# Row maximum of two steps ahead placed in front of the lower half of the probabilities, on VectorE, in the steps that make no scores

## The chip, the cores and the metric

One core of one Trainium2 chip runs the whole program. The metric is the device time of one execution in microseconds (us). Three executions of the kernel before took 634.48, 625.78 and 636.51 us: median 634.48. "Faster" and "slower" below mean by more than 2%.

## The reference, cut to what matters

A gated cross attention is followed by a gated feed-forward part. The attention is where the change lies:

```python
x = rmsnorm(layernorm(x)); q = x @ wq.T; k = ctx @ wk.T; v = ctx @ wv.T      # 16 heads of 32
attn = einsum('blhd,bmhd->bhlm', q, k) * 32**-0.5
attn = where(mask, attn, -inf); attn = softmax(attn)
out = einsum('bhlm,bmhd->blhd', attn, v) @ wo.T
x = x + tanh(g_xattn) * sigmoid(x @ wg.T) * out
```

x is 16 batches of 100 tokens by 512; the context has 361 rows for each batch, of which this path of the kernel reads the last 96 (the mask lets only those through; it looks first whether that holds). The feed-forward part has 1408 hidden units, with weights kept as 4-bit codes that VectorE decodes during the attention.

## The kernel before, in words

The 16 batches are taken in 4 groups of 4. The attention of a group is 16 **steps**, one for each head; a step is done for the 4 batches at once. Groups 0 to 2 from step 6 on, with steps 0 to 5 of the next group, are one pass of a loop that runs three times (called a cycle here); steps 0 to 5 of group 0 stand ahead of it, steps 6 to 15 of group 3 behind it. Each engine has its own list of instructions in the order written and goes through it in that order; semaphores alone tie the engines.

For head n = 16g + i, `step(g, i)` does on each engine:

- TensorE: transposes the probabilities of head i (`bank<-ident,probs`, L1584, three instructions; it waits for `exp` of head i and for `pT_lo` of the step before), multiplies the transposed probabilities of head i-1 by the values (`attend`, L1597, nine instructions; it waits for `pT_lo` of i-1 and for `o` of i-2), in steps with i % 4 == 2 makes the scores of the four heads that follow at i+2 to i+5 (`scores`, L1563 and L1573), and then runs the step's jobs from the table `BESIDE`.
- ScalarE: `probsT_hi` (L880) copies the transposed probabilities rounded to `pT_hi`; `exp_step` (L872, `probs<-bank,nmax`, four instructions) makes the exponentials of head i+2, for which it needs the row maximum `nmax` of that head; then the upper halves of the jobs (`vb_hi`, `kT_hi`, `qT_hi`, `xT_hi`, `oT_hi`).
- VectorE: `probsT_lo` (L1127) makes `pT_lo`, what the rounding left over; `attn_norm` (L1135 `rinv`, L1137 `o`) divides the result of head i-1; `row_max` (L1122, `nmax`) takes the negated row maximum of head i+2; `decode` pieces (`words`, `fp`, `left`, `scale`); then the lower halves of the jobs (`kT_lo` and so on), each of which waits for its upper half from ScalarE.

Each of TensorE's products is done in three passes (hi*hi, hi*lo, lo*hi), which is why every operand has two halves. `scores` writes banks 2 to 5. Before it does so it waits for what used each bank last; for bank 2 that is a job T (turned `o`) whose last reader is `oT_lo`, and in steps 14 and 2 for bank 3 a job X or B (`vb_lo`). A job's name says what it is: X turned tokens, Q, K projections, A and B values, G gate, T turned attention result, O output projection.

In the last group, steps 11 to 15 also run the first tiles of the feed-forward part (L1693 on TensorE, `part_gate` and `part_up` on ScalarE L959 and VectorE L1320). Their products go to the scores' banks 2 to 4, and each bank is opened when `exp` of the head that last held it is done (`open_bank_of`).

The `row_max` of a step reads scores that were made in a step with i % 4 == 2, for heads i+2 to i+5: in that same step only the first of the four is taken, in the three steps that follow the other three.

Of the kernel before, what the change touches and what calls it, by code (L numbers as in the profile page):

```python
# [22 lines left out]
HPG = HEADS // HG  # L23
# [37 lines left out]
def build(nc, x, ctx_tail, ctx_full, mask, mask_tail, g_xattn, g_ffn, norm_w, wq, wk, wv, wo, wg,  # L61
          packed, gu_scales, dn_scales, identity, shifts, x1_dram, gu_dram, dn_dram, out):
    es = ExitStack()
    with es:
# [277 lines left out]
        LOOP_FROM, AHEAD, SCORES_AT = 6, 2, 2  # L342
# [71 lines left out]
        def beside(g, i):  # L414
            jobs = [(g + (i >= LOOP_FROM and IN_STEPS.index(n) >= IN_STEPS.index("X0")), n) for n in BESIDE[i]]
            return [job for job in jobs if exists(*job)]

        def step_ahead(g, i):
            g, i = (g, i + AHEAD) if i + AHEAD < STEPS else (g + 1, i + AHEAD - STEPS)
            return [(g, i)] if not isinstance(g, int) or g < GROUPS else []  # L420
# [8 lines left out]
        def last_step(g, i):  # L429
            return (g, i - 1) if i else (g - 1, STEPS - 1)  # L430
# [638 lines left out]
        def _(dve):  # L1069
# [50 lines left out]
            def row_max(g, i):  # L1120
                dve.wait_ge(s_sc, STEPS * g + i + 1)
                nc.vector.tensor_reduce(nmax[:, i % 4, :], SC[i % HPG][0:L, 0:KC].rearrange("t (b k) -> t b k", b=NB),  # L1122
                                        AXIS_X, ALU.max, negate=True).then_inc(s_max, 1)

            def probsT_lo(g, i):
                dve.wait_ge(s_pthi, STEPS * g + i + 1)
                nc.vector.tensor_tensor(pT[i % 2][LO][:, :, :].rearrange("k c t -> k (c t)"), PT[:, 0:CHUNKS * L],  # L1127
                                        pT[i % 2][HI][:, :, :].rearrange("k c t -> k (c t)").bitcast(F32), ALU.subtract)\
                  .then_inc(s_ptlo, 1)
# [21 lines left out]
            def step(g, i, last=False, cycle=None):  # L1151
                def dequant(place):
                    if cycle is not None:
                        for q, stage in DECODE_AT.get((i, place), ()):
                            decode(cycle, q, stage)

                probsT_lo(g, i)
                dequant(0)
                if not isinstance(g, int) or g or i:
                    attn_norm(*last_step(g, i))  # L1160
                for ahead in step_ahead(g, i):
                    row_max(*ahead)
                dequant(1)
                if not last:
                    for b in NORM_AT.get(i, ()):
                        layer_stats(g + 1, b)
                if last and i == STATS_AT:
                    for m in range(3):
                        ffn_stats(0, m)
                for c, name in beside(g, i):  # L1170
                    if name[0] == "O":
                        output(c - 1, int(name[1]))
                    elif name[0] != "G":
                        job_lo(c, name)
                if not last:
                    for b in NORM_AT.get(i - 1, ()):
                        normalise(g + 1, b)
                dequant(2)
                if last and i in NORMED_AT:
                    if i == min(NORMED_AT):  # L1180
                        dve.wait_ge(s_ctxlo, KT * GROUPS)
                    ffn_normalise(0, NORMED_AT[i])
                if last and i in TURNED_AT:
                    mT_lo(0, TURNED_AT[i])
                if last and i in FIRST_AT:
                    ffn_tile(0, FIRST_AT[i])
# [681 lines left out]
```

## Time and profile before

| | us |
|---|---|
| three executions | 625.78, 634.48, 636.51 |
| median | 634.48 |
| profiled execution, span from first to last instruction | 633.5 |
| TensorE busy | 586.4 |
| VectorE busy | 467.0 |
| ScalarE busy | 324.2 |
| mean granted TensorE clock, share of full speed | 0.936 |

The profiled execution is one execution. Its own time is known as its span; it is 1.0 us below the median of the three. The attention takes the first 375 us or so of it, the rest is the feed-forward part, in which no instruction that the change moves is left. TensorE's busy time is modelled, since its matmuls overlap: a short wait of it can be hidden in it. In a timeline row the number in square brackets is how long the engine stood idle just before, and behind the arrow is what ended the wait.

### The profile page before, as it was taken

How to read it: one execution, taken by the hardware profiler on the slowest of the kernel's cores; microseconds unless marked ns; L12 is line 12 of the kernel's file. 1: busy time of each engine (PE TensorE's matmuls, PEld its weight loads, DVE VectorE, ACT ScalarE, POOL GpSimd, SP SyncE). 2: the span in 40 equal slices, each digit the busy share in tenths (PEclk: the TensorE clock that was granted, in tenths of full speed). 3: DMA queues.
4: the chain of work that ended last, by engine and by line, in shares of the span. 5: the costliest groups of instructions: out<-in, count | busy, mean ns of one | idle time of the engine just before them, and what ended most of it. 6: DMA issues, size and time to landing. Idle time of an engine off the chain costs nothing.

```text
span 633.5 us, 12518 instructions
## 1 busy us (share of the span) xinstructions
PE 586.4 (93%) x4154; PEld 516.0 (81%) x4154; DVE 467.0 (74%) x1063; ACT 324.2 (51%) x872; POOL 227.3 (36%) x244
## 2 busy tenths in 40 slices
PE   3988999999999999998998889899999998999996
PEld 2888878888789788887887877788888897899983
DVE  6466977857877579686655698899889789877731
ACT  4665454433454434553345563666765665666620
POOL 6811130001120001300000363576766676776730
PEclk9787987999897899897999799899999999999999
DMA  7910135232344321342258002820111210011010
GB/s 236 319 70 1 64 129 166 100 103 78 124 128 157 92 78 50 119 121 99 78 194 304 4 2 79 300 74 20 57 34 34 76 35 0 35 35 34 34 60 29
DMA packets 27900, 59.38 MB, mean 94 GB/s; under 512 B 3657, under 2 KB 5833, under 8 KB 27849
## 3 DMA queue, kind: packets, MB, share of 16 engines
q1 hardware_dynamic: 27848, 58.76, 28.3%
q8 instruction: 24, 0.39, 0.3%
q14 instruction: 28, 0.22, 0.1%
HBM read 39.62 MB, written 19.14 MB: 93 GB/s over the span
## 4 chain that ended last, share of the span: by engine, by line
PE 53%; DVE 23%; ACT 9%; issue 8%; POOL 5%; DMA 0%; DVEq 0%; SPq 0%; ACTq 0%; POOLq 0%
PE bank L1693 14%; PE bank L317 11%; PE bank L1706 11%; PE bank L1545 5%; PE bank L1573 3%; PE bank L1597 3%; ACT probs L872 3%; PE bank L1549 3%; DVE pT_lo L1127 2%; DVE vb_lo L1090 2%; POOL hT_lo L753 2%; DVE part_gate L1320 2%; DVE nmax L1122 2%; DVE hidden L1335 1%; PE bank L1584 1%
## 5 line engine op out<-in xcount | busy, mean ns | idle before, releaser
L1693 PE MATMUL bank<-mT_hi,wgu 128*128 128x320 f32 x440 | 142.2, 333 | 14.4 <-DVE part_up L1320 4.9
L1693 PE MATMUL bank<-mT_lo,wgu 128*128 128x320 f32 x440 | 135.3, 318 | 0.0
L872 ACT ACTIVATE probs<-bank,nmax 100x96 f32<-100x96 f32 x256 | 66.2, 341 | 124.0 <-DVE nmax L1122 123.9
L1693 PEld LDWEIGHTS bank<-mT_hi,wgu 128*128 128x128 f32 x440 | 85.7, 195 | 28.4 <-DVE part_up L1320 7.8
L1693 PEld LDWEIGHTS bank<-mT_lo,wgu 128*128 128x128 f32 x440 | 86.1, 196 | 3.4
L760 POOL TENSOR_TENSOR part_gate<-part_gate 128x320 f32<-128x320 f32 x55 | 57.0, 1037 | 80.7 <-DVE part_gate L1320 80.7
L959 ACT ACTIVATE part_up<-bank,scale 128x320 f32<-128x320 f32 x110 | 57.3, 521 | 48.6 <-PE bank L1693 48.5
L1320 DVE SCALAR_TENSOR_TENSOR part_up<-bank,scale,part_up 128x320 f32<-128x320 f32 x110 | 58.5, 545 | 19.9 <-ACT part_up L959 17.0
L959 ACT ACTIVATE part_gate<-bank,scale 128x320 f32<-128x320 f32 x110 | 52.2, 528 | 28.4 <-PE bank L1693 27.6
L1320 DVE SCALAR_TENSOR_TENSOR part_gate<-bank,scale,part_gate 128x320 f32<-128x320 f32 x110 | 55.3, 543 | 13.9 <-ACT part_gate L959 11.3
L766 POOL TENSOR_TENSOR part_up<-part_up 128x320 f32<-128x320 f32 x55 | 57.0, 1037 | 23.6 <-DVE part_up L1320 22.1
L703 POOL TENSOR_TENSOR rstd<-var,halfpow 100x1 f32<-100x1 f32 x16 | 9.2, 573 | 144.0 <-DVE var L1112 143.9
L1706 PE MATMUL bank<-wdn_lo,hT_hi 128*128 128x512 f32 (+1 forms) x143 | 56.6, 396 | 0.0
L1706 PE MATMUL bank<-wdn_hi,hT_lo 128*128 128x512 f32 (+1 forms) x143 | 56.5, 395 | 0.0
L1706 PE MATMUL bank<-wdn_hi,hT_hi 128*128 128x512 f32 (+1 forms) x143 | 56.4, 395 | 0.0
L753 POOL TENSOR_TENSOR hT_lo<-hidden,hT_hi 128x320 fp32r<-128x320 f32 x55 | 49.5, 899 | 4.8 <-ACT hT_hi L973 3.9
L1597 PE MATMUL bank<-vb_hi,pT_hi 128*100 128x68 f32 x192 | 50.8, 265 | 0.0
L1597 PE MATMUL bank<-vb_lo,pT_hi 128*100 128x68 f32 x192 | 50.7, 264 | 0.0
L1597 PE MATMUL bank<-vb_hi,pT_lo 128*100 128x68 f32 x192 | 50.6, 264 | 0.0
L1122 DVE TENSOR_REDUCE nmax<-bank 100x4 f32<-100x384 f32 x64 | 35.2, 549 | 6.8 <-PE bank L1573 6.8
L1127 DVE TENSOR_TENSOR pT_lo<-bank,pT_hi 128x300 fp32r<-128x300 f32 x64 | 29.9, 467 | 7.7 <-ACT pT_hi L880 6.8
L1090 DVE TENSOR_TENSOR vb_lo<-bank,vb_hi 32x256 fp32r<-32x256 f32 (+2 forms) x56 | 23.6, 422 | 16.2 <-ACT vb_hi L852 15.4
(145 smaller groups left out, 1498.0 us busy)
## 6 DMA issues: line engine op xcount, KB each, us to landing
gate_up_scratch<-left SPq DMA_DIRECT2D x12, 512.0 KB, 5.4
down_scratch<-left SPq DMA_DIRECT2D x12, 512.0 KB, 3.8
wgu<-gate_up_scratch SPq DMA_DIRECT2D x11, 512.0 KB, 7.6
words<-in_packed SPq DMA_DIRECT2D x18, 256.0 KB
xn<-in_x SPq DMA_DIRECT2D x16, 200.0 KB
xa<-in_x SPq DMA_DIRECT2D x16, 200.0 KB
x_scratch<-gate SPq DMA_DIRECT2D x16, 200.0 KB
ctx_raw<-in_ctx_tail SPq DMA_DIRECT2D x4, 768.0 KB, 7.8
```

Of the source, the lines that this page charges most:

```text
L317: last = nc.tensor.matmul(out_ap, lhs(a, t), rhs(b, t), start=t == 0 and p == 0, stop=t == tiles - 1 and p == 2)
L753: nc.gpsimd.tensor_tensor(hT[t][LO][:, cols], hidden[n % 2][:, :], hT[t][HI][:, cols].bitcast(F32), ALU.subtract)\
L760: nc.gpsimd.tensor_tensor(a[:, :], a[:, :], b[:, :], ALU.add).then_inc(s_gate_sum, 1)
L766: nc.gpsimd.tensor_tensor(a[:, :], a[:, :], b[:, :], ALU.add).then_inc(s_up_sum, 1)
L872: last = nc.scalar.activation(probs[i % 2][:, cols], SC[i % HPG][0:L, cols], ACT.Exp, bias=nmax[:, i % 4, b:b + 1])
L959: nc.scalar.activation(part[n % 2][i][k][:, :], product_bank(j, t, i, k)[:, 0:TG], ACT.Copy, scale=scale32[:, t, i, k:k + 1]).then_inc(s_e ...
L1122: nc.vector.tensor_reduce(nmax[:, i % 4, :], SC[i % HPG][0:L, 0:KC].rearrange("t (b k) -> t b k", b=NB), AXIS_X, ALU.max, negate=True).the ...
L1127: nc.vector.tensor_tensor(pT[i % 2][LO][:, :, :].rearrange("k c t -> k (c t)"), PT[:, 0:CHUNKS * L], pT[i % 2][HI][:, :, :].rearrange("k c ...
L1320: nc.vector.scalar_tensor_tensor(onto, product_bank(j, t, i, k)[:, 0:TG], scale32[:, t, i, k:k + 1], onto, ALU.mult, ALU.add).then_inc(s_e ...
L1597: last = nc.tensor.matmul(PV[0:L, VW * c:VW * c + 2 * VW].rearrange("t (b w) -> t b w", w=VW), pT[i % 2][ph][:, c, :], vb[vh][:, c, :, VW ...
L1693: last = nc.tensor.matmul(product_bank(j, t, i, k)[:, 0:TG], wgu[t][:, k, 128 * i:128 * i + 128], mT[j % 2][half][:, k, :], start=half == ...
L1706: last = nc.tensor.matmul(bank[6 + slot][0:rows, :], hT[c][a][:, cols], wdn[c][b][:, :], start=c == 0 and p == 0, stop=c == FT - 1 and p == 2)
```

## The change

In steps with i % 4 != 2 (`SCORES_AT` is 2, `HPG` is 4) VectorE now runs `row_max` ahead of `probsT_lo`; before, it ran behind `attn_norm`. In steps with i % 4 == 2 it stays where it was. Nothing is added or taken away, and no other engine's list changes.

```diff
+                if i % HPG != SCORES_AT:
+                    for ahead in step_ahead(g, i):
+                        row_max(*ahead)
                 probsT_lo(g, i)
                 dequant(0)
                 if not isinstance(g, int) or g or i:
                     attn_norm(*last_step(g, i))
-                for ahead in step_ahead(g, i):
-                    row_max(*ahead)
+                if i % HPG == SCORES_AT:
+                    for ahead in step_ahead(g, i):
+                        row_max(*ahead)
                 dequant(1)
```

The first place is VectorE in the loop, steps 12 and 13 (`nmax` is the row maximum, `pT_lo` the lower half, `fp`, `words` and `left` are decoding). Before:

```order
L1099 TENSOR_TENSOR kT_lo<-bank,kT_hi 128x384
L1127 TENSOR_TENSOR pT_lo<-bank,pT_hi 128x300
L1135 RECIPROCAL rinv<-bank 100x4
L1137 TENSOR_TENSOR o<-bank,rinv 100x4x32
L1121 REGISTER_ALU
L1122 TENSOR_REDUCE nmax<-bank 100x4
L1243 REGISTER_ALU
L1249 CAST left<-fp 128x1024
L1227 TENSOR_SCALAR words<-words,shift 128x512
L1085 REGISTER_ALU
L1096 SCALAR_TENSOR_TENSOR qT_lo<-bank,qT_hi 128x400
L1127 TENSOR_TENSOR pT_lo<-bank,pT_hi 128x300
```

With the change (lines below the edit are four further down):

```order
L1099 TENSOR_TENSOR kT_lo<-bank,kT_hi 128x384
L1121 REGISTER_ALU
L1122 TENSOR_REDUCE nmax<-bank 100x4
L1127 TENSOR_TENSOR pT_lo<-bank,pT_hi 128x300
L1135 RECIPROCAL rinv<-bank 100x4
L1137 TENSOR_TENSOR o<-bank,rinv 100x4x32
L1247 REGISTER_ALU
L1253 CAST left<-fp 128x1024
L1231 TENSOR_SCALAR words<-words,shift 128x512
L1085 REGISTER_ALU
L1096 SCALAR_TENSOR_TENSOR qT_lo<-bank,qT_hi 128x400
L1121 REGISTER_ALU
```

The row maximum moved past three instructions, to the place right behind the job of the step before; the decoding and the jobs stand in the same order as they did.

The second place is VectorE in the last group, step 12, beside the first feed-forward tiles (`part_gate`, `part_up`, `hidden`). Before:

```order
L1328 SCALAR_TENSOR_TENSOR hidden<-tgate,part_gate 128x320
L1127 TENSOR_TENSOR pT_lo<-bank,pT_hi 128x300
L1135 RECIPROCAL rinv<-bank 100x4
L1137 TENSOR_TENSOR o<-bank,rinv 100x4x32
L1122 TENSOR_REDUCE nmax<-bank 100x4
L1320 SCALAR_TENSOR_TENSOR part_gate<-bank,scale,part_gate 128x320 x2
```

With the change:

```order
L1332 SCALAR_TENSOR_TENSOR hidden<-tgate,part_gate 128x320
L1122 TENSOR_REDUCE nmax<-bank 100x4
L1127 TENSOR_TENSOR pT_lo<-bank,pT_hi 128x300
L1135 RECIPROCAL rinv<-bank 100x4
L1137 TENSOR_TENSOR o<-bank,rinv 100x4x32
L1324 SCALAR_TENSOR_TENSOR part_gate<-bank,scale,part_gate 128x320 x2
```

Here it moved past the wait of `rinv` for TensorE's `attend` as well, behind which it stood before.

## Rows read from the trace of the kernel before

**Rows 1.** The page, part 1: busy time of each engine, its share, instructions.

```profile
PE 586.4 (93%) x4154; PEld 516.0 (81%) x4154; DVE 467.0 (74%) x1063; ACT 324.2 (51%) x872; POOL 227.3 (36%) x244
```

**Rows 2.** Waits of TensorE, whole span: total us, times, longest us.

```profile
PE bank L1563 <- DVE oT_lo L1101: 8.6, 9, 1.4
PE bank L1563 <- DVE vb_lo L1090: 3.1, 4, 1.6
PE bank L1584 <- DVE pT_lo L1127: 2.0, 1, 2.0
```

**Rows 3.** Waits, 60 to 365 us: ScalarE's exponentials.

```profile
ACT probs L872 <- DVE nmax L1122: 114.5, 57, 3.2
```

**Rows 4.** Timeline of VectorE, third cycle: start, us, [idle before].

```profile
262.33 0.47 DVE L1127 TENSOR_TENSOR pT_lo<-bank,pT_hi 128x300 fp32r<-128x300 f32 x1 [0.56 <-ACT pT_hi L880]
...
268.96 0.57 DVE L1096 SCALAR_TENSOR_TENSOR qT_lo<-bank,qT_hi 128x400 fp32r<-128x400 f32 x1 [0.49 <-ACT qT_hi L858]
...
270.25 0.55 DVE L1122 TENSOR_REDUCE nmax<-bank 100x4 f32<-100x384 f32 x1
...
272.29 0.57 DVE L1101 TENSOR_TENSOR oT_lo<-bank,oT_hi 128x400 fp32r<-128x400 f32 x1 [0.43 <-ACT oT_hi L862]
```

**Rows 5.** Timeline of ScalarE, step 13 of that cycle.

```profile
270.83 1.03 ACT L872 ACTIVATE probs<-bank,nmax 100x96 f32<-100x96 f32 x4 [1.59 <-DVE nmax L1122]
```

**Rows 6.** Timeline of TensorE, third cycle: where scores open their banks.

```profile
254.10 0.55 PE L1563 MATMUL bank<-mb,ones 1*100 1x384 bf16 x4 [0.86 <-DVE oT_lo L1101]
...
272.92 0.45 PE L1563 MATMUL bank<-mb,ones 1*100 1x384 bf16 x4 [1.38 <-DVE oT_lo L1101]
...
291.50 0.36 PE L1563 MATMUL bank<-mb,ones 1*100 1x384 bf16 x1 [1.21 <-DVE oT_lo L1101]
...
292.34 0.45 PE L1563 MATMUL bank<-mb,ones 1*100 1x384 bf16 x3 [0.48 <-DVE vb_lo L1090]
```

**Rows 7.** Timeline of VectorE: steps 7, 15 and 1 before those waits.

```profile
239.19 0.47 DVE L1127 TENSOR_TENSOR pT_lo<-bank,pT_hi 128x300 fp32r<-128x300 f32 x1 [0.33 <-ACT pT_hi L880]
...
281.35 1.28 DVE L1090 TENSOR_TENSOR vb_lo<-bank,vb_hi 32x256 fp32r<-32x256 f32 x3 [0.58 <-ACT vb_hi L852]
...
290.40 0.56 DVE L1099 TENSOR_TENSOR kT_lo<-bank,kT_hi 128x384 fp32r<-128x384 f32 x1 [0.62 <-ACT kT_hi L860]
```

**Rows 8.** Timeline of ScalarE and TensorE ahead of the loop.

```profile
40.48 1.03 ACT L872 ACTIVATE probs<-bank,nmax 100x96 f32<-100x96 f32 x4 [1.42 <-DVE nmax L1122]
...
43.47 0.37 PE L1563 MATMUL bank<-mb,ones 1*100 1x384 bf16 x3 [1.61 <-DVE vb_lo L1090]
```

**Rows 9.** Timeline of TensorE and ScalarE in the last group, steps 11 to 13.

```profile
346.22 0.41 PE L1693 MATMUL bank<-mT_hi,wgu 128*128 128x320 f32 x1 [1.50 <-ACT probs L872]
...
352.26 1.03 ACT L872 ACTIVATE probs<-bank,nmax 100x96 f32<-100x96 f32 x4 [1.98 <-DVE nmax L1122]
...
353.77 0.63 PE L1693 MATMUL bank<-mT_hi,wgu 128*128 128x320 f32 x1 [0.79 <-ACT part_gate L959]
...
361.31 0.42 PE L1693 MATMUL bank<-mT_hi,wgu 128*128 128x320 f32 x1 [1.35 <-ACT part_gate L959]
```

**Rows 10.** Tightest place of `pT_lo` before the next transposes, VectorE then TensorE.

```profile
277.89 0.47 DVE L1127 TENSOR_TENSOR pT_lo<-bank,pT_hi 128x300 fp32r<-128x300 f32 x1
...
278.51 0.45 PE L1584 MATMUL bank<-ident,probs 100*128 100x100 f32 x3
```

**Rows 11.** Windows: stretch, length, busy of PE, PEld, DVE, ACT, POOL, PEclk, DMA share, GB/s.

```profile
184.53:206.83 22.30, 20.91 (x179) 20.67 (x178) 17.54 (x40) 10.66 (x35) 0.00 (x0) 0.77 0.48 146
270.37:289.13 18.76, 16.97 (x179) 16.25 (x178) 16.83 (x39) 9.67 (x32) 0.00 (x0) 1.00 0.43 136
...
206.83:215.11 8.28, 7.33 (x78) 5.50 (x77) 4.56 (x10) 2.97 (x10) 0.00 (x0) 0.79 0.22 71
289.13:299.56 10.43, 8.74 (x78) 6.52 (x77) 5.18 (x12) 3.71 (x13) 0.00 (x0) 0.69 0.12 50
342.78:362.82 20.04, 16.40 (x90) 14.72 (x89) 11.91 (x29) 11.55 (x33) 5.20 (x6) 0.74 0.27 81
```

## The prediction

> **What bounds the kernel now.** I read the page's part 1 first: TensorE is busy 93% of the span, VectorE 74%, ScalarE 51% [rows 1]. The change takes nothing from TensorE's work, so all it can give back is time in which TensorE waits, or works at a lower clock. Second, TensorE's waits [rows 2]: the largest that this change can reach is the one before the scores, 8.6 us in 9 times for `oT_lo` and 3.1 us in 4 times for `vb_lo`, then one of 2.0 us for `pT_lo`. Third, who holds VectorE and ScalarE up: in the attention ScalarE's exponentials wait 57 times for the row maximum, 114.5 us together, about 2 us each [rows 3]. That wait alone costs nothing, since the head is needed only two steps later. It costs because ScalarE is strictly in order: the upper halves of the jobs stand behind the exponentials, and VectorE needs them for its lower halves, and then stands idle itself. The timelines show this circle. In the third cycle `qT_lo`, `oT_lo`, `vb_lo` and `kT_lo` each waited for their upper half, 0.49, 0.43, 0.58 and 0.62 us [rows 4, 7], and at the end of each such run of steps TensorE waits for VectorE: 1.38 us in step 14, 1.21 and 0.48 us in step 2, 0.86 us in step 10 [rows 6]. So from step 11 to step 2 the pace is set by VectorE and ScalarE in turn, not by TensorE.
>
> **What the change does to one step.** VectorE's own sum is untouched: the same row maximum of 0.55 us stands 0.7 us earlier (in step 13 `qT_lo` ends at 269.53 and the row maximum starts at 270.25 [rows 4]). What is gained is overlap. The exponentials, which began at 270.83 [rows 5], can begin when the row maximum in front is done, about 269.53 + 0.5, so 0.7 to 0.8 us earlier; `oT_hi` behind them ends as much earlier, and the idle 0.43 us of VectorE before `oT_lo` [rows 4] goes. An idle time of VectorE goes in full if it is below that 0.7 us, and every one listed above is. Where VectorE stood idle for `pT_hi` itself, the row maximum runs inside that idle time: of the 0.56 us before `pT_lo` in step 11 [rows 4] it fills 0.47, of the 0.33 us in step 7 [rows 7] all.
>
> **The sum of the waits.**
> - Step 14, three cycles. VectorE's idle times on the way from step 11 are 0.47 (the part filled) + 0.49 + 0.43 = 1.39 us [rows 4], against TensorE's wait of 1.38 us [rows 6]. All of it goes: 3 x 1.38 = 4.1 us.
> - Step 10, three cycles. VectorE runs without a pause from step 7 to `oT_lo`, so the 0.33 us filled in step 7 [rows 7] comes straight off the 0.86 us [rows 6]: 3 x 0.33 = 1.0 us.
> - Step 2, three cycles. In the third 0.58 + 0.62 = 1.20 us [rows 7] off 1.69 us of waits [rows 6]; in the first two TensorE is slower in steps 14 and 15, and only the 0.62 us in front of the scores counts: 1.2 + 2 x 0.62 = 2.4 us.
> - Ahead of the loop. ScalarE's wait of 1.42 us before `exp` in step 1 [rows 8] goes nearly whole, since there VectorE has nothing in front of the row maximum; with the work in order behind it, some 1.3 of the 1.61 us at 43.47 [rows 8] go. The 2.0 us wait for `pT_lo` [rows 2] loses little, because the row maximum now stands before that very `pT_lo`: 0.2. Together 1.5 us.
> - Last group, steps 11 to 13. TensorE waits 1.50 us for `exp` itself, and 0.79 and 1.35 us for `part_gate`, which stands behind `exp` on ScalarE [rows 9]. In step 12 the row maximum stood behind the wait for `attend`, hence ScalarE's 1.98 us [rows 9]; in front it waits for nothing. I take 0.9 (the row maximum in front of `pT_lo` and `o`, as above) + 0.8 (all) + 1.0 = 2.7 us.
>
> Sum: 4.1 + 1.0 + 2.4 + 1.5 + 2.7 = 11.7 us.
>
> **What it costs.** `pT_lo` now stands behind 0.47 us of row maximum where VectorE arrives late (34 of the 47 changed steps by the timeline), and with it `rinv` and `o` of the step before. TensorE needs `pT_lo` at the next transposes. The tightest place is step 15 of the third cycle: `pT_lo` ends at 278.36, the transposes start at 278.51 [rows 10]; there the 0.47 us is paid. In 41 of the 47 steps there are more than 0.6 us between, and at step 13, where there are 0.45, VectorE arrives 0.9 us earlier. I take one such payment in each cycle, 3 x 0.47 = 1.4 us; the ends are 0 and, if all 34 paid, 16. No DMA moves: VectorE issues none, and SP waits for decoding steps that keep their places. The scores that the row maximum reads were finished a step before, so it brings no new wait of its own. Net of waits: 11.7 - 1.4 = 10.3 us.
>
> **The clock.** TensorE's clock falls from 2.4 to 1.2 GHz after such waits. Steps 14 to 1 take 22.30 us in the second cycle at a granted 0.77 and 18.76 us in the third at 1.00, after the same wait of 1.38 us; the stretch behind it takes 8.28 us at 0.79 and 10.43 us at 0.69 [rows 11]. So a full clock in one stretch gave 3.5 us, of which 2.1 were lost again in the next: net 1.4. The last group's 20.04 us ran at 0.74 [rows 11], that is 20.04 x 0.26 = 5.2 us of lost pulses. Without the waits in front part of this comes back. The upper end is 2 x 3.5 + 5.2 = 12.2 us; the lower end is a loss, since shorter waits elsewhere can meet the clock worse: 2 x 2.1 = 4.2 us, the way the third cycle's step 2 did. I take 2 x 1.4 and a little of the last group, 3.2 us, nearer to what the third cycle netted than to the end. The Trainium skill (Perfetto Trace Analysis, Matmul Optimizations) says that the matmul engine scales with utilization, so that back-to-back batches matter. The trace agrees in kind; by the rule alone I would have moved toward the upper end, some 611 us.
>
> Together 10.3 + 3.2 = 13.5 us. Against the profiled execution's own 633.5 us that is 620.0; this execution lies 1.0 us below the median of the three, so for the median: **621.0 us**. A measurement can tell about 2%, 12.7 us, from no change: the line lies at 621.8, and the forecast sits on it.
>
> **The rivals.**
> - *The clock comes back whole* (16%). For it: every stretch at a lowered clock in the attention begins behind one of the waits that shrink [rows 6, 9, 11]. Against: waits of 0.5 us in step 10 and over 0.5 us in step 2 stay. Time: 634.5 - 10.3 - 12.2 = 612.
> - *`pT_lo` takes the place of the waits* (20%). The circle of ScalarE and VectorE gets shorter, but TensorE, already at 93% [rows 1], then waits for `pT_lo` at the transposes or is simply the bound, and half of the 10.3 us arrives and no clock: 629.5. For it: rows 10, and 0.15 us of room at the worst place.
> - *No effect* (4%). The Trainium skill (Perfetto Trace Analysis, Identifying the Most-Contended Engine) says to improve the engine with the highest occupancy. As a mechanism here: TensorE is that engine by rows 1, the order on VectorE would be hidden under it, and the time stays 634.5. The trace speaks against it with TensorE's 11.7 us of named waits in rows 2.
> - *Slower* (5%). `pT_lo` and `attend` are late in every step where VectorE arrives after `pT_hi`: 34 x 0.47 = 16 us, with nothing gained because the upper halves turn out to wait for TensorE's jobs rather than for the exponentials. 650 at the worst; it decides over 2% from 27 steps that pay. The 41 steps with over 0.6 us of room speak against it.
>
> **How the numbers follow.** The forecast's case has 55%, with 614 to 628 of its own (the clock's ends cut to what is likely, and the payments 0 to 3); half of it lies below 621.8. Faster by over 2%: 0.28 + 0.16 and a little = 0.45. Slower: 0.05. Within 2%: 0.50. The range of 610 to 632 leaves out the slower case, most of no effect, and the outer ends of the two others, under 2 in 10.
>
> **What would show it.** Right: in the list of waits ScalarE's wait for the row maximum falls from 114.5 us to under 40; TensorE's wait for `oT_lo` falls from 8.6 us to 2 to 4, gone in step 14, near 0.5 us in step 10; the waits of 1.50, 0.79 and 1.35 us in the last group shrink to under 0.7 us each; VectorE's busy time stays at 467. The clock term shows in the windows as a granted clock above 0.77 in steps 14 to 1 of the first two cycles. Wrong: a new line of TensorE waiting for `pT_lo` or `o` over 3 us, or upper halves that now wait for TensorE with `oT_lo` as late as before. If the waits fall as said and the time does not, the step that failed is the clock.

## The result: 612.6 us against 631.0, in the predicted range

| | before | after |
|---|---|---|
| median of four executions | 631.03 us (625.78 to 636.51) | 612.56 us (611.13 to 613.51) |
| profiled execution, span | 633.5 us | 610.4 us |
| its mean granted TensorE clock | 0.936 | 0.968 |

The ratio is 0.9722, with a 95% interval of 0.9672 to 0.9772: faster by 2.3 to 3.3%. The medians differ by 18.5 us. The forecast was 621.0 in a range of 610 to 632. The result lies outside the 614 to 628 of the forecast's own case; the case nearest to it is the rival "the clock comes back whole", 612. Ratios, here and below, leave out executions over 1.5% above the fastest of their kernel (three of the ten of e3, for instance), while medians and ranges are over all.

The page of the changed kernel, part 1 (answers to [rows 1]). VectorE has the same work (468.5 us after 467.0). TensorE is busy for 17 us less with the same 4154 instructions, while its mean granted clock rose from 0.936 to 0.968; since its busy time is modelled and can hide short waits, I don't put all of the 17 down to the clock.

```profile
PE 569.5 (93%) x4154; PEld 498.4 (82%) x4154; DVE 468.5 (77%) x1063; ACT 325.9 (53%) x872; POOL 226.0 (37%) x244
```

Waits of TensorE in the changed kernel, whole span: total us, times, longest us (answers to [rows 2]; lines below the edit are four further down). The wait before the scores (L1567) for `oT_lo` fell from 8.6 to 2.7 us, for `vb_lo` from 3.1 to 1.7. New is a wait for `pT_lo` at the transposes (L1588), three times 0.44. The single one of 1.98 us for `pT_lo` ahead of the loop is not in this execution; e1 and e12, which have the same order there, show it again with 1.92, so the order did not remove it.

```profile
PE bank L1567 <- DVE oT_lo L1101: 2.7, 8, 0.5
PE bank L1697 <- ACT part_gate L959: 2.3, 2, 1.2
PE bank L1567 <- DVE vb_lo L1090: 1.7, 4, 0.5
PE bank L1588 <- DVE pT_lo L1127: 1.3, 3, 0.4
PE bank L1697 <- ACT probs L872: 0.7, 1, 0.7
```

ScalarE's wait for the row maximum, 60 to 345 us, which is the same part of the program as 60 to 365 was (answers to [rows 3]): 78.3 us, not the "under 40" that I had named.

```profile
ACT probs L872 <- DVE nmax L1122: 78.3, 51, 3.5
```

The circle of the two engines in steps 12 to 14 of the third cycle: VectorE first, then ScalarE (answers to [rows 4, 5]). The row maximum now stands ahead of `pT_lo`; ScalarE waits 0.80 us for it in step 13, where it waited 1.59; VectorE waits 0.23 us for `qT_hi` where it waited 0.49, and not at all before `oT_lo`.

```profile
249.50 0.54 DVE L1122 TENSOR_REDUCE nmax<-bank 100x4 f32<-100x384 f32 x1
249.97 0.45 DVE L1127 TENSOR_TENSOR pT_lo<-bank,pT_hi 128x300 fp32r<-128x300 f32 x1
...
252.06 0.57 DVE L1096 SCALAR_TENSOR_TENSOR qT_lo<-bank,qT_hi 128x400 fp32r<-128x400 f32 x1 [0.23 <-ACT qT_hi L858]
252.55 0.55 DVE L1122 TENSOR_REDUCE nmax<-bank 100x4 f32<-100x384 f32 x1
...
254.86 0.57 DVE L1101 TENSOR_TENSOR oT_lo<-bank,oT_hi 128x400 fp32r<-128x400 f32 x1
```

```profile
253.13 1.04 ACT L872 ACTIVATE probs<-bank,nmax 100x96 f32<-100x96 f32 x4 [0.80 <-DVE nmax L1122]
```

TensorE in steps 10, 0 and 2 of the third cycle (answers to [rows 6, 10]); step 14 has no wait there now, and one of 0.15 us in the two cycles before. Then its three waits in the last group (answers to [rows 9]): 0.68, 1.13 and 1.17 us, which were 1.50, 0.79 and 1.35.

```profile
237.86 0.55 PE L1567 MATMUL bank<-mb,ones 1*100 1x384 bf16 x4 [0.47 <-DVE oT_lo L1101]
...
261.53 0.45 PE L1588 MATMUL bank<-ident,probs 100*128 100x100 f32 x3 [0.44 <-DVE pT_lo L1127]
...
272.92 0.36 PE L1567 MATMUL bank<-mb,ones 1*100 1x384 bf16 x1 [0.35 <-DVE oT_lo L1101]
273.69 0.45 PE L1567 MATMUL bank<-mb,ones 1*100 1x384 bf16 x3 [0.41 <-DVE vb_lo L1090]
```

```profile
326.53 0.42 PE L1697 MATMUL bank<-mT_hi,wgu 128*128 128x320 f32 x1 [0.68 <-ACT probs L872]
...
332.20 0.41 PE L1697 MATMUL bank<-mT_hi,wgu 128*128 128x320 f32 x1 [1.13 <-ACT part_gate L959]
...
338.12 0.41 PE L1697 MATMUL bank<-mT_hi,wgu 128*128 128x320 f32 x1 [1.17 <-ACT part_gate L959]
```

Windows (answers to [rows 11]; the columns are the same, the one before the last two is the granted clock): steps 14 to 1 of cycles 1 and 3, step 2 of the three cycles, and steps 11 to 13 of the last group. Steps 14 to 1 took 22.30 us at 0.77 in the first two cycles and 18.76 at 1.00 in the third; they take 17.25 at 1.00 in all three. Step 2 keeps the full clock in the first cycle alone: 6.53 us, against 9.65 and 9.58 at 0.65.

```profile
95.27:112.50 17.23, 16.64 (x178) 16.13 (x177) 16.25 (x38) 9.85 (x32) 0.00 (x0) 1.00 0.58 183
254.17:271.41 17.24, 16.65 (x179) 16.15 (x178) 16.26 (x38) 9.87 (x32) 0.00 (x0) 1.00 0.46 149
112.50:119.03 6.53, 5.77 (x79) 4.54 (x78) 4.88 (x12) 2.66 (x9) 0.00 (x0) 1.00 0.19 42
189.61:199.26 9.65, 8.89 (x79) 6.71 (x77) 4.88 (x12) 2.67 (x9) 0.00 (x0) 0.65 0.22 68
271.41:280.99 9.58, 8.82 (x79) 6.59 (x78) 4.87 (x12) 2.66 (x9) 0.00 (x0) 0.65 0.14 55
...
323.90:328.95 5.05, 4.37 (x31) 3.57 (x30) 2.82 (x8) 3.76 (x11) 0.74 (x1) 1.00 0.97 290
328.95:334.20 5.25, 4.12 (x30) 3.44 (x28) 4.16 (x11) 3.60 (x11) 1.96 (x3) 1.00 0.07 25
334.20:339.64 5.44, 4.27 (x35) 3.78 (x33) 4.47 (x12) 3.96 (x13) 2.54 (x4) 1.00 0.00 0
```

**How the time is split.** A step's length is the distance between the starts of two transposes of probabilities on TensorE. All steps that the table leaves out are equal in both kernels to 0.1 us in the second cycle (heads 22 to 37). "Old order" at the full clock is the kernel before with its waits filled (e4 below).

| step | before, cycle 2 | old order, full clock (e4) | after, cycle 1, full clock | after, cycle 2 |
|---|---|---|---|---|
| 10 | 8.28 | 6.60 | 6.30 | 6.31 |
| 14 | 7.75 | 5.39 | 4.25 | 4.28 |
| 15 | 4.61 | 2.76 | 3.10 | 3.09 |
| 0 | 4.97 | 4.90 | 4.91 | 4.91 |
| 1 | 4.97 | 5.72 | 4.97 | 4.97 |
| 2 | 8.28 | 7.38 | 6.53 | 9.65 |

The two middle columns give what the order is worth with the clock taken out: 32.75 - 30.06 = 2.7 us a cycle, **8.1 us** in three. e4 has useless matmuls and another order of banks in it; put together from stretches without them at the full clock (step 10 and step 2 in e2, 6.70 and 7.44; steps 14 to 1 in the third cycle of before, 18.76), the old order takes 32.9, and the order is worth 8.5. Ahead of the loop, steps 0 to 5 went from 29.55 us at a granted 0.83 to 27.32 at 0.75, **2.2** (clock included). In the last group no run has steps 11 to 13 in the old order at 1.00 in one piece; single steps at 1.00 give 18.2 us (5.85, 6.10 and 6.23 us in e2, e3 and e3), and the new order takes 15.74: **2.4**. Together 12.7 us by order. The two profiles differ by 23.1 us, so some 10.4 are left for the clock; the medians differ by 18.5, so 5.8 are.

The 10.4 can be found again in the profiles. For each stretch this is the time above its length at the full clock in the same order, three cycles together:

| stretch | full clock, old order | above it, before | full clock, new order | above it, after |
|---|---|---|---|---|
| step 10 | 6.70 | 4.7 | 6.30 | 1.6 |
| steps 14 to 1 | 18.76 | 7.1 | 17.24 | 0 |
| step 2 | 7.44 | 4.4 | 6.53 | 6.2 |

The clock gave back 3.1 us in step 10 and 7.1 in steps 14 to 1, and took 1.7 in step 2; in the last group it gave 1.8 (20.04 against 18.2). That is 10.3, where the order, at 8.5 or 8.1 in the loop, leaves 10.0 or 10.4. These are net costs: a stretch at half clock has shorter waits in it, because TensorE comes later to them.

The 5.8 can be had in a second way. The kernel before ran 37 times in all beside the experiments, from 625.92 us at a mean granted clock of 0.963 to 637.66 at 0.936. A straight line through the 37 gives 0.29 us for each us that TensorE spends at half clock (2 x (1 - clock) x span; correlation 0.93). The median execution of before has 57 us of it, of after 39: 18 x 0.29 = 5.2 us.

### The profile page after: what moved, and what is told of

Its sections match the earlier page's. It is cut to its first block, busy times and chain, and to the rows that moved or that the text cites. A ratio compares the mean times of both kernels' runs of the same rounds, so it can differ in the third digit from the quotient of the medians.

```text
span 610.4 us, 12518 instructions
## 1 busy us (share of the span) xinstructions
PE 569.5 (93%) x4154; PEld 498.4 (82%) x4154; DVE 468.5 (77%) x1063; ACT 325.9 (53%) x872; POOL 226.0 (37%) x244
## 4 chain that ended last, share of the span: by engine, by line
PE 55%; DVE 24%; issue 9%; POOL 6%; ACT 5%; DVEq 1%; DMA 0%; SPq 0%; ACTq 0%; POOLq 0%
PE bank L1697 14%; PE bank L1710 11%; PE bank L317 10%; PE bank L1549 6%; PE bank L1601 4%; PE bank L1553 3%; PE bank L1577 3%; POOL hT_lo L753 2%; DVE nmax L1122 2%; DVE part_gate L1324 2%; DVE vb_lo L1090 2%; PE bank L326 2%; DVE stats L1107 2%; DVE pT_lo L1127 2%; DVE hidden L1339 1%
## 5 line engine op out<-in xcount | busy, mean ns | idle before, releaser
L1697 PE MATMUL bank<-mT_hi,wgu 128*128 128x320 f32 x440 | 139.9, 328 | 14.2 <-DVE part_up L1324 4.9
L1697 PE MATMUL bank<-mT_lo,wgu 128*128 128x320 f32 x440 | 132.0, 310 | 0.0
L1697 PEld LDWEIGHTS bank<-mT_hi,wgu 128*128 128x128 f32 x440 | 82.9, 188 | 30.0 <-DVE part_up L1324 8.0
L1697 PEld LDWEIGHTS bank<-mT_lo,wgu 128*128 128x128 f32 x440 | 83.2, 189 | 3.5
L973 ACT ACTIVATE hT_hi<-hidden 128x320 fp32r<-128x320 f32 x55 | 25.7, 468 | 18.8 <-DVE hidden L1339 18.7
L880 ACT ACTIVATE pT_hi<-bank 128x300 fp32r<-128x300 f32 x64 | 26.9, 420 | 15.4 <-PE bank L1588 14.9
```

What stands on the lines that cost most here:

```text
L1697: last = nc.tensor.matmul(product_bank(j, t, i, k)[:, 0:TG], wgu[t][:, k, 128 * i:128 * i + 128], mT[j % 2][half][:, k, :], start=half == ...
```

## The experiments

Each verdict is a ratio to the kernel before on the same chip, with its 95% interval. The executions of before had medians of 629.5 to 631.1. At the 2% line e8 to e12 are faster and e3 and e5 the same. e1, e2, e4, e6 and e7 are unclear: their intervals lie below 1, so each is faster than before, but reach above 0.98. Differences of a few us between two experiments are within these intervals, and where I use them I go by the lengths in the traces.

**e1: the changed kernel without its three busiest steps**

```diff
-                if i % HPG != SCORES_AT:
+                first = i % HPG != SCORES_AT and (cycle is None or i not in (11, 12, 13))
+                if first:
                     for ahead in step_ahead(g, i):
                         row_max(*ahead)
...
-                if i % HPG == SCORES_AT:
+                if not first:
```

> The changed kernel with the old order put back in steps 11, 12 and 13 of the loop only. Theory (the wait and the clock it brings down): TensorE's wait of about 1.38 us before the scores of step 14 returns in all three cycles, 4.1 us in waits, and the granted clock falls again behind it in some of them, so steps 14 to 1 go from about 17.2 us to 19 to 22 us; the whole is 6 to 12 us slower than the changed kernel, 619 to 625 us. Rival (waits alone, the clock is chance): the 4.1 us return and no more, 616.5 us. Rival (the gain lies in the last group and ahead of the loop): within 2 us of the changed kernel.

616.84 us (615.09 to 621.56), ratio 0.9804 [0.9703, 0.9904]: 4.3 above the changed kernel, and the wait of step 14 is back, 1.39 us in all three cycles. The interval is too wide to tell 4.3 from the 6 to 12 that I expected, but the three cycles of the two profiles differ by 4.5. That is close to the waits' 4.1 with no clock on top, my first rival. The windows of steps 14 to 1 in the three cycles show why "no clock" isn't "the clock did not move":

```profile
94.43:113.04 18.61, 16.64 (x179) 16.14 (x177) 17.16 (x39) 10.84 (x36) 0.00 (x0) 1.00 0.54 171
174.44:194.36 19.92, 18.13 (x179) 17.59 (x177) 17.16 (x39) 10.97 (x36) 0.00 (x0) 0.91 0.54 162
257.37:278.16 20.79, 19.39 (x179) 19.16 (x177) 17.26 (x39) 11.06 (x36) 0.00 (x0) 0.84 0.37 125
```

The same wait of 1.39 us led to 1.00, 0.91 and 0.84. What the third cycle lost there (3.55 us against after) it won back but for 0.5 in step 2, which took 6.53 us where the changed kernel takes 9.58.

**e2: only those three steps, in the loop**

```diff
+                first = i % HPG != SCORES_AT and (cycle is not None and i in (11, 12, 13))
...
```

> The kernel before with the new order in steps 11, 12 and 13 of the loop only. Theory: the 1.38 us wait of step 14 goes in all three cycles and with it the half-clock stretch that followed it in two of them: 4.1 us of waits and 3 to 7 us of clock, 620 to 624 us against 631. Rival (waits alone): 627 us. Rival (the order must change in every step, since the circle of the two engines is one): the wait of step 14 stays above 0.7 us and the time within 2 us of the kernel before.

619.03 us (616.21 to 625.25), 0.984 [0.973, 0.9951]: 12.0 us from three steps. The order gives 3 x 1.2 (step 14 waits 0.15); the rest goes with the clock: steps 14 to 1 run at 1.00 in all three cycles, 17.4 us each. At the full clock the old order of the other steps shows its whole waits, those of steps 1 and 2 of the first cycle:

```profile
112.86 0.39 PE L317 MATMUL bank<-wv_hi,ctxT_hi 128*128 128x256 f32 x1 [0.43 <-DVE vb_lo L1090]
...
116.76 0.36 PE L1568 MATMUL bank<-mb,ones 1*100 1x384 bf16 x1 [1.21 <-DVE oT_lo L1101]
117.59 0.44 PE L1568 MATMUL bank<-mb,ones 1*100 1x384 bf16 x3 [0.47 <-DVE vb_lo L1090]
```

2.11 us a cycle, and the two waits of step 2 are the same in all three; in the profile of before only the third cycle, the one at full clock, had them. In the second cycle step 2 itself stays at the full clock here, which gives its length in the old order, 7.44 us:

```profile
196.13:203.57 7.44, 5.76 (x78) 4.53 (x77) 5.17 (x12) 3.69 (x13) 0.00 (x0) 1.00 0.10 29
```

e1 and e2 are the change in two parts, and together they gain 26 us, more than the whole change's 18.5: part of the clock comes back with either of them, and it comes back only once.

**e3: the other way to break the circle, ScalarE's exponentials behind its upper halves**

```diff
                 probsT_hi(g, i)
-                for ahead in step_ahead(g, i):
-                    exp_step(*ahead)
+                if last:
+                    for ahead in step_ahead(g, i):
+                        exp_step(*ahead)
                 for job in beside(g, i):
                     if job[1][0] != "O":
                         job_hi(*job)
+                if not last:
+                    for ahead in step_ahead(g, i):
+                        exp_step(*ahead)
```

> The kernel before, VectorE's order untouched; on ScalarE the exponentials stand behind the upper halves of the step's jobs instead of in front of them, except in the last group. Theory (what cost was that the upper halves stood behind the exponentials, which wait for the row maximum): VectorE's idle times before qT_lo, kT_lo, oT_lo and vb_lo fall as they do in the changed kernel, TensorE's wait in step 14 falls from 1.38 to under 0.5 us, and the time comes to 612 to 622 us although the row maximum is where it was. Rival (what counts is the earlier row maximum and earlier exponentials themselves): no gain or slower, 631 us or more, since the exponentials now come later than before.

630.09 us (622.8 to 635.57), 0.9958 [0.9899, 1.0018]: no gain, where I had expected 612 to 622. Steps 14 to 1 got shorter (19.10, 20.44 and 18.30 us after 22.29, 22.30 and 18.76), but steps 6 to 13 went from 37.7 us to 40.6, 42.2 and 39.1. TensorE there, steps 7, 10 and 11: it now waits for the exponentials' bank, and the wait of step 10 has grown.

```profile
149.64 0.45 PE L317 MATMUL bank<-xT_hi,wq_hi 128*128 128x400 f32 x1 [0.69 <-ACT probs L872]
165.31 0.55 PE L1567 MATMUL bank<-mb,ones 1*100 1x384 bf16 x4 [1.38 <-DVE oT_lo L1105]
173.49 0.56 PE L1528 MATMUL bank<-ident,xn 100*128 100x100 f32 x4 [0.74 <-ACT probs L872]
```

**e7: the same, in steps 11 to 15, 0 and 1 alone**

```diff
-                if last:
+                if last or 2 <= i <= 10:
...
-                if not last:
+                if not last and not 2 <= i <= 10:
```

(Shown against e3.)

> The kernel before, VectorE's order untouched; ScalarE runs the exponentials behind the step's upper halves in steps 11 to 15, 0 and 1 only (in the run with it in every step, TensorE came to wait for exponentials in steps 7, 11 and 15, up to 0.9 us). Theory (upper halves behind the exponentials were the cause): VectorE's idle times before qT_lo, oT_lo, vb_lo and kT_lo go in these steps, TensorE's wait in step 14 falls from 1.38 to 0.9 or less and the one in step 2 from 1.69 to under 0.9 us, steps 7 to 10 stay as before; 618 to 626 us. Rival (only the earlier row maximum helps): TensorE's waits in steps 14 and 2 stay and the time is 631.

622.0 us (620.47 to 625.08), 0.9849 [0.9771, 0.9927]. The wait of step 14 fell less than with the row maximum in front, to 0.91 us, those of step 2 a little more, to 0.47. Step 10 keeps its old wait of 0.86 us and runs at 1.00 in all three cycles all the same (6.70 us, before 8.28 at 0.79); most of the gain of e7 is clock, in steps 10 and 2. In steps 14 to 1 the lowered clock followed the 0.91 in all three cycles:

```profile
98.99:120.94 21.95, 21.01 (x178) 20.62 (x177) 17.76 (x42) 10.21 (x32) 0.00 (x0) 0.77 0.50 152
180.91:202.87 21.96, 21.02 (x178) 20.63 (x177) 17.76 (x42) 10.21 (x32) 0.00 (x0) 0.77 0.48 151
262.83:284.79 21.96, 21.02 (x178) 20.63 (x177) 17.76 (x42) 10.21 (x32) 0.00 (x0) 0.77 0.34 115
```

So the circle can be opened from both sides: with VectorE's order untouched, the waits of steps 14 and 2 shrink as soon as the upper halves no longer stand behind the exponentials. The change takes the side that costs little elsewhere, 0.44 us at one transpose in each cycle.

**e5: the new order outside the loop alone**

```diff
+                first = i % HPG != SCORES_AT and (cycle is None)
...
```

> The new order only where it is not in the loop: ahead of it and in the last group. Theory: the stretch ahead of the loop is 2 us shorter and steps 11 to 13 of the last group 4 us shorter, as in the changed kernel; the loop's waits of 1.38 us (step 14) and 0.86 us (step 10) stay: 623 to 626 us. Rival (the loop gave everything, the last group's gain was only its luck with the clock): within 2 us of the kernel before, with steps 11 to 14 of the last group at 22 us or more.

627.83 us (622.69 to 630.78), 0.9948 [0.9903, 0.9994]: 2.2 us in the medians, short of the 623 to 626 us that I had expected. The interval, 0.4 to 6.1 us, holds the 4.6 us (2.2 and 2.4) that the split above gives to the two ends, and does not confirm it. In the profile steps 11 to 13 of the last group are as in the changed kernel (the last four counted steps 19.83 us, after 19.82, before 24.13). The lowered clock in the loop, 0.77 in steps 14 to 1 of the first cycle, stayed.

**e6: the row maximum one place further back, between `pT_lo` and `attn_norm`**

```diff
+                probsT_lo(g, i)
                 if i % HPG != SCORES_AT:
                     for ahead in step_ahead(g, i):
                         row_max(*ahead)
-                probsT_lo(g, i)
                 dequant(0)
```

> The changed kernel with the row maximum one place later: behind the lower half of the probabilities and in front of the division of the step before, so that the lower half is never held up by it. Theory: the exponentials start 0.4 us earlier than in the kernel before instead of 0.7 to 0.8, the idle 0.47 us of VectorE in steps 7 and 11 is not filled, so TensorE's wait in step 14 comes to 0.3 to 0.7 us and in step 10 stays at 0.86 us; the new wait of 0.44 us for the lower half in step 0 goes. 615 to 621 us. Rival (holding up the lower half is a real cost, and it outweighs the earlier exponentials): 612 us or less.

615.26 us (612.44 to 616.52), 0.9735 [0.9657, 0.9813]; the interval holds the changed kernel's ratio. The time is at the lower end of the 615 to 621 us expected. The wait at step 0 is there all the same, 0.43 us, now for `o`. e10 settles it.

**e4: the kernel before, its waits filled with useless matmuls.** In the steps that make scores, TensorE opens banks 4 and 5 first, which are free, and writes into bank 4 matmuls that the real ones overwrite: 8 in steps 14 and 2, 4 in step 10, from the loop on. VectorE's and ScalarE's order is the old one. The edit does two things, it fills and it opens the banks as 4, 5, 2, 3; e11 below tells them apart.

```diff
-                for h in range(HPG):
+                fill = {0: 8, 1: 8, 3: 4}.get(hg, 0) if not isinstance(g, int) or g else 0
+                for h in (2, 3, 0, 1):
                     open_bank(g + 1 if f"S{hg}" in OF_LAST else g, f"S{hg}", 2 + h)
+                    for _ in range(fill if h == 2 else 0):
+                        nc.tensor.matmul(SC[h][0:L, 0:KC], W["wq"][HI][:, 0, 0:L],
+                                         W["wq"][HI][:, 1, 0:KC], start=True, stop=True)
```

> The kernel before, with TensorE kept at work during its wait before the scores: in the loop, ahead of the scores of steps 14 and 2 eight extra matmuls of 384 columns (four ahead of step 10), into the bank of the third head, whose result the next matmul overwrites; the four banks are opened in the order 4, 5, 2, 3, so that the filling runs while bank 2 is still held. VectorE's and ScalarE's order is the old one. Theory (the wait costs twice, once as waiting and once as clock): the stop in front of bank 2 ends no earlier, but the granted clock of steps 14 to 1 stays near 1.00 in all three cycles and 3 to 6 us are gained over the whole, 625 to 628 us. Rival (the clock has nothing to do with the waits): the granted clock stays near 0.77 in steps 14 to 1 of two cycles and the time is 631 to 634 us, up to 3 us longer where the filling was longer than the wait.

619.11 us (616.66 to 620.48), 0.9815 [0.9722, 0.9908]: 12 us faster for 64 matmuls that compute nothing, where I had expected 3 to 6. The products of queries and keys start no earlier than `oT_lo` and `vb_lo` let them, only the mask products (`mb`, `ones`) of banks 4 and 5 move ahead of the wait; the windows (steps 14 to 1 of the third cycle, step 2 of the second and third) show the clock whole, and the old order's waits inside the lengths:

```profile
256.46:275.25 18.79, 18.26 (x187) 17.33 (x186) 16.85 (x39) 9.69 (x32) 0.00 (x0) 1.00 0.42 136
195.47:202.85 7.38, 7.06 (x87) 5.62 (x86) 5.19 (x12) 3.72 (x13) 0.00 (x0) 1.00 0.10 31
275.25:282.60 7.35, 7.04 (x87) 5.61 (x85) 5.18 (x12) 3.70 (x13) 0.00 (x0) 1.00 0.01 3
```

**e8 and e12: the changed kernel with its waits filled,** 4 matmuls in step 2, 3 in step 10; the rest of the edit is as in e4.

```diff
+                fill = {1: 4, 3: 3}.get(hg, 0) if not isinstance(g, int) or g else 0
...
```

> The changed kernel with TensorE kept at work in the two waits before scores that it still has: four extra matmuls of 384 columns ahead of the scores of step 2, three ahead of those of step 10, into the third head's bank, whose result the next matmul overwrites. Theory (the wait costs again in clock): the granted clock stays at 1.00 from step 7 to step 5 in all three cycles; half-clock stretches behind step 2 (two cycles, 9.6 us for a step that takes 6.5 at full clock) and step 10 (one cycle, 1.6 us) go: 3 to 7 us faster than the changed kernel, 606 to 610 us. Rival (the clock falls elsewhere instead, or the fill itself costs what it saves): 612 us.

> The kernel of e8 once more, beside e9 to e11 on the same chip and in five rounds: 604 us again (602.6 to 605.0 before), with the clock 1.00 in steps 14 to 1 and in step 2 of all three cycles. If e8 had been luck of one chip, it would now lie nearer to the changed kernel's 612.6.

604.1 us (602.59 to 605.0), 0.9565 [0.9492, 0.9639], and again 603.8 us (602.63 to 604.84), 0.959 [0.9547, 0.9633]. It beats both kernels. Step 2 of the three cycles in e12, with 4 matmuls more than after:

```profile
111.48:117.92 6.44, 6.36 (x83) 4.96 (x81) 4.88 (x12) 2.66 (x9) 0.00 (x0) 1.00 0.19 49
188.36:194.81 6.45, 6.37 (x83) 4.96 (x82) 4.89 (x12) 2.67 (x9) 0.00 (x0) 1.00 0.07 25
265.27:271.70 6.43, 6.35 (x82) 4.95 (x81) 4.88 (x12) 2.65 (x9) 0.00 (x0) 1.00 0.01 4
```

Against the changed kernel step 2 gained 3.2 us in the second and 3.15 in the third cycle, and steps 6 to 13 of the third 1.7: 8.0, and the medians differ by 8.8. From e4 to e8, both filled, the medians differ by 15.0 us: 12.7 of order, and the rest I put down to clock that the fill does not reach.

**e11: as many useless matmuls in a cycle (7), but where TensorE hardly waits** (4 in step 6, 3 in step 14)

```diff
+                fill = {0: 3, 2: 4}.get(hg, 0) if not isinstance(g, int) or g else 0
...
```

> The changed kernel with as many useless matmuls as e8, but elsewhere: 4 before the scores of step 6, where TensorE waits for nothing, and 3 before those of step 14, where it waits 0.15 us. If filling the waits is what kept the clock (my theory), step 2 still goes on at half clock after its two waits, and the 7 matmuls of 0.15 us each (at full clock) are a plain addition of about 1 us a cycle, 3 us in all: 612 to 616 us against the changed kernel's 612.6. Rival: any more work on TensorE keeps its clock, wherever it stands: then 604 to 606 us, as e8, with the clock 1.00 in step 2 of all cycles.

610.13 us (609.24 to 613.52), 0.9693 [0.9647, 0.974], apart from e12's interval and not from the changed kernel's. Step 10 of the first cycle, and step 2 of the second and third:

```profile
79.53:87.33 7.80, 7.60 (x82) 5.85 (x81) 4.94 (x9) 3.14 (x10) 1.96 (x2) 0.78 0.60 184
192.83:202.39 9.56, 9.09 (x79) 6.79 (x78) 4.88 (x12) 2.66 (x9) 0.00 (x0) 0.64 0.22 73
275.44:281.87 6.43, 5.96 (x78) 4.57 (x77) 4.88 (x12) 2.67 (x9) 0.00 (x0) 1.00 0.01 4
```

e11 opens the banks in e12's order too, in every step that makes scores. Steps 10 and 2 have that order here and no useless matmul in them, and the clock falls in step 10 of two cycles (7.80 and 7.83 us) and in step 2 of one. So the order of the banks alone doesn't hold the clock; what it gives is about 0.1 us in a step (step 2 at full clock 6.43, after 6.53). On the old order of VectorE it was not run alone. The useless matmuls pay most in the waits. But the rival that any more work helps isn't wholly refuted: the matmuls add 1.0 us a cycle in steps 6 and 14, and the time is no longer for it, with a mean clock of 0.970 to 0.984 in its executions against 0.968 to 0.974 of after. A wait of 0.40 us before step 2's scores stood in both rows; one lost the clock, one didn't.

**e9 and e10: what `pT_lo` pays,** at a clock of 1.00 in steps 10 and 14 to 2 of all cycles. e9 is e8's kernel with step 15 in e6's order, e10 with all steps in it.

```diff
-                if i % HPG != SCORES_AT:
+                if i % HPG != SCORES_AT and i != 15:
...
                 probsT_lo(g, i)
+                if i == 15:
+                    for ahead in step_ahead(g, i):
+                        row_max(*ahead)
                 dequant(0)
```

> The kernel of e8 (the new order, with 4 useless matmuls before the scores of step 2 and 3 before those of step 10), except that in step 15 the row maximum goes back behind pT_lo (ahead of attn_norm). It asks for the price of holding up pT_lo, which the prediction put at 0.47 us in each cycle. If that is a real cost: TensorE's wait of 0.44 us for pT_lo at step 0 goes, three times, and the time falls by up to 1.3 us against e8's kernel. Rival: the reciprocal and the product of attn_norm are then late instead, and TensorE waits for o at step 0 as it did in e6 (0.43 us): no change. I expect the rival, 604 us.

> The kernel of e8 with the row maximum between pT_lo and attn_norm in every step that makes no scores, instead of in front of pT_lo. e6 was 2.7 us above the changed kernel's median, but with a lower clock in some stretches. With the clock near full, only the waits are left: step 14's wait before the scores grows from 0.15 to 0.27 us, step 10's from 0.1 to about 0.3, step 2's from nothing to 0.3: about 0.7 us a cycle, and 1 us in the last group, so 2 to 3 us above e8, 606 to 607. Rival: place between the two makes no difference, and e6's 2.7 us was clock alone: 604.

e9: 604.25 us (602.22 to 605.53), 0.9591 [0.9547, 0.9635], the same as e12. Its step 15 is 0.6 us shorter (2.59 against 3.17), its step 0 is 0.46 longer, step 2 0.25 longer; TensorE waits for `o` at `attend` instead:

```profile
181.14 0.25 PE L1607 MATMUL bank<-vb_hi,pT_hi 128*100 128x68 f32 x1 [0.43 <-DVE o L1137]
```

e10: 609.93 us (607.62 to 610.69), 0.9678 [0.9633, 0.9722]: 6 us above e12, twice what I expected. In the loop it is 0.9 us a cycle (steps 10, 14, 15, 0 and 2: 25.80 us together, in e12 24.90). Another 0.8 us is in the last group, where the waits are 1.07, 1.53 and 0.67 us. The profiled execution's first 33 us, ahead of everything that differs, take 2.3 us more, and the part behind the attention 1.0; neither belongs to the order, and I can't name their cause. The first stretch varies without any edit: in e8 and e12, which are one kernel, it took 32.5 and 31.0 us.

## Why the prediction was right, point by point

- **VectorE and ScalarE set the pace in turn: right.** Moving either engine's item (the change, e7) shortens TensorE's wait in step 14. My sign for it was wrong: ScalarE's wait for `nmax` was to fall under 40 us and fell to 78.3. It is 36 us shorter over some 50 waits, 0.7 us each (0.79 in step 13), which is what the row maximum moved, and the rest of the 2 us was never in reach of the change. A wait that costs nothing was a poor witness.
- **Step 14, 4.1 us: right, a little too large.** The wait went from 1.38 to 0 or 0.15; the step at full clock from 5.49 (before, third cycle) to 4.26, 3.7 us in three. The cycles of e1, which has the wait again, are 4.5 us longer together.
- **Step 10, 1.0 us: right.** 0.86 to 0.47, the step 0.3 shorter each time.
- **Step 2, 2.4 us: right,** 0.85 a cycle at the full clock, 2.6. The way to it was not: I took the smaller waits of the first two cycles, which were only small because TensorE came late at half clock. At full clock all three have 1.21 + 0.47 (e2). The third of them was read rightly.
- **Missing: step 1.** A wait of 0.41 us for `vb_lo` in front of a job, once in the profile of before, in the cycle at full clock:

```profile
287.60 0.39 PE L317 MATMUL bank<-wv_hi,ctxT_hi 128*128 128x256 f32 x1 [0.41 <-DVE vb_lo L1090]
```

  It was in all three cycles as soon as the clock was back, and the step is 0.75 us longer by it: 2.3 us that the sum lacked.
- **The hold-up of `pT_lo`, 3 x 0.47 = 1.4 us: right in size and place.** Three waits of 0.44 at step 0, step 15 longer by 0.34 to 0.45; the 34 feared payments did not come. e9 shows that one place further back doesn't avoid it: `o` is then as late.
- **Ahead of the loop 1.5, measured 2.2; last group 2.7, measured 2.4.** The 1.61 us for `vb_lo` went to 0.47 (the forecast left 0.3 of it). With the step behind them, steps 0 to 6 take 34.8 to 35.2 us in the old order (before, e2, e4) and 31.5 to 32.9 in the new (after, e1, e5, e12), so 2.2 is at the low end there. The named sign failed there too (each wait under 0.7 us; two are 1.13 and 1.17). The steps are shorter by the predicted amount, but TensorE, now at full clock, arrives earlier at what is left.
- **Waits and order together:** predicted 10.3 us, measured 12.7.
- **The clock, 3.2 us, is the term that was mis-sized.** It is 5.2 to 5.8 us in the medians and 10.4 between the two profiles, near the upper end of 12.2 that I had set and thought unlikely. For steps 14 to 1 the forecast counted 2 x 3.5 = 7.0 us, and 7.1 came. It then took 2 x 2.1 off again for step 2. Step 2 did pay: in the new kernel it runs at half clock in two cycles, 3.1 us each, behind waits of 0.35 and 0.41 us. But it had paid 4.4 us before too, so the difference is 1.7 and not 4.2. Step 10 had no term at all and gave 3.1 us: its clock was 0.79 in all three cycles of before and is 1.00, 1.00 and 0.78 now. Its own shorter wait needn't be the reason, since in e7 it ran at 1.00 three times behind the old wait. The last group gave 1.8 us, where the sum had 0.4 and the upper end 5.2; most of the 5.2 us of missing clock had cost no time. e4, with the old order of VectorE and ScalarE, prices the clock at some 12 us.
- **The base.** The profiled execution of before ran at 0.936, the median one at 0.955. The sum of waits was rightly taken from it; a clock term has to be taken from the median's clock, and then the most that the clock can give is smaller than 12.2. A span is also 2.3 us shorter than the time of the same execution (610.4 and 612.71 us for the changed kernel), so the profiled execution of before was some 1.3 us above the median of the three, not 1.0 below it. The forecast doesn't change by that, since it comes to 634.5 - 13.5 either way. The median of before is 631.03 with the fourth execution: from there the same 13.5 us would have given 617.5, and 5.0 of the 8.4 us between forecast and result are left.
- **Luck.** The range held, but the forecast's own case did not: its terms were 2.4 us short in the order and 2.0 to 2.6 short in the clock in the medians, and the range reached to 610 only for the sake of a rival that had 16%. The kernel before varies by 12 us between executions, so a median of three or four could as well have moved the base the other way.

The Trainium skill (TensorE: Matmul & The Clock Gate, A second HAM failure mode: psum-queue depth-cycling) describes a kernel in which short idle times between groups of matmuls make the clock go to and fro, with a cost between the groups at each return; its kernel goes through the PSUM banks in turn. The rows of steps 10, 14 and 2 agree in kind: half clock sets in behind waits of 0.4 to 1.4 us, in some cycles and not in others. No run here shows what decides it.

## What to carry to other kernels

On in-order engines, a result that is needed late but opens another engine's queue belongs at the front of its own queue: look at what stands behind the waiting instruction, not at the wait. Where the clock is lowered behind short waits of TensorE, first price the clock alone, by filling the waits with matmuls that nobody reads, before arguing about it; it takes a few lines and here it was worth 8 us on top of the change. Waits that were read at half clock are too small, and some don't show at all: read them in a repetition of the loop that ran at full clock.

## What the runs showed of the hardware that I had not expected

- Useless matmuls in TensorE's waits made the kernel before 12 us faster (e4) and the changed one 8.8 us (e12). In the waits they cost nothing visible: step 2 takes 6.44 us with four of them and 6.43 to 6.53 without, at full clock. Elsewhere seven of them add 1.0 us (e11).
- The same wait can be followed by a full or a half clock: 1.39 us by 1.00, 0.91 and 0.84 in three cycles of one execution (e1), 0.40 us by 0.64 and 1.00 (e11), but 0.91 us by 0.77 three times (e7); 0.86 us in step 10 by 0.79 three times in before and by 1.00 three times in e7. Half clock costs 3.1 us in step 2, 1.6 to 1.7 in step 10, and 4.2 in steps 14 and 15 together.
- Most of the spread between executions of one kernel is this clock: 37 executions of before lie between 625.9 us at 0.963 and 637.7 us at 0.936; the 10 of e8 and e12, at 0.983 to 0.992, lie between 602.6 and 605.0.
